# Twelve batches' block flags kept from the counting pass for the sort, and the accumulator zeroed by one transfer

## The reference

```python
xn = layernorm(x)
# graph: messages weighed by edge_weight, added up by their target node
support = xn @ gnn_weight
agg = segment_sum(edge_weight[:, None] * support[dst], src, 6250)
g = relu(agg + gnn_bias + xn)
x = x + g + linear_attention_block(xn)        # 8 heads, feed-forward 1024
x = x + top2_of_8_experts(layernorm(x))       # 256 -> 512 -> 256
```

## Time and profile before

| | us |
|---|---|
| median of 3 runs (lowest, highest) | 3451.71 (3448.81, 3453.6) |
| the profiled execution's own time | 3441.95 |
| its span | 3440.2 |
| PE busy (share of the span) | 2606.8 (76%) |
| DVE busy | 2346.8 (68%) |
| POOL busy | 2226.2 (65%) |
| ACT busy | 1248.0 (36%) |

### The profile page before, as it was taken

One profiled execution on the slowest core, in us unless ns is written; L12 is line 12 of the kernel. 1 busy time (PEld: TensorE's weight loads), 2 busy tenths in 40 slices (PEclk: granted clock), 3 DMA queues, 4 the chain that ended last, 5 costly groups with the idle time before them and its releaser, 6 DMA issues.

```text
span 3440.2 us, 46797 instructions
## 1 busy us (share of the span) xinstructions
PE 2606.8 (76%) x10870; PEld 1931.2 (56%) x10870; DVE 2346.8 (68%) x5310; ACT 1248.0 (36%) x2681; POOL 2226.2 (65%) x2110
## 2 busy tenths in 40 slices
PE   5888888667877786786786787787688754888886
PEld 2677777545544454564554565555555533776775
DVE  7999999745555656657656656656656657877863
ACT  0111111045444343344344343343344423444532
POOL 2355555577777777777777777777777733554552
PEclk9666666579889888988898998898898965999998
DMA  3111110065453543453554544445444386555445
GB/s 126 39 34 34 34 34 26 12 127 121 119 125 111 118 117 115 124 121 117 123 119 122 118 119 124 119 116 127 115 107 116 111 185 219 132 130 135 104 87 117
DMA packets 418876, 370.29 MB, mean 108 GB/s; under 512 B 248648, under 2 KB 357232, under 8 KB 418256
## 3 DMA queue, kind: packets, MB, share of 16 engines
q0 software_dynamic: 105424, 247.55, 28.0%
q1 hardware_dynamic: 304720, 110.37, 13.6%
q10 hardware_dynamic: 8496, 9.75, 0.8%
HBM read 299.09 MB, written 74.81 MB: 109 GB/s over the span
## 4 chain that ended last, share of the span: by engine, by line
PE 23%; DVE 20%; issue 12%; POOL 9%; DVEq 7%; DMA 6%; SPq 1%; ACT 1%; POOLq 0%; ACTq 0%
POOL rows L766 8%; DVE R L1567 8%; PE ps L929 6%; DVEq L1561 5%; PE ps L1003 5%; PE ps L995 4%; PE ps L1053 3%; DMA total<-y_w,zt 2%; DMA rows<-support,t_dst 2%; DVEq L1567 1%; DMA zt<-routed 1%; PE ps L963 1%; DVE xnT L1627 1%; DVE is_low L1554 1%; DVE stats L1482 1%
## 5 line engine op out<-in xcount | busy, mean ns | idle before, releaser
L766 POOL DMA_INDIRECT rows<-support,t_dst x1624 | 1598.5, 984 | 503.3 <-issue 462.7
L929 PE MATMUL ps<-rows,hot 128*128 128x256 f32 x3248 | 927.5, 435 | 377.9 <-DVE R L1567 259.8
L1567 DVE TENSOR_TENSOR R<-R,ps 128x256 f32 x1624 | 683.2, 421 | 754.3 <-DVE R L1567 474.8
L929 PEld LDWEIGHTS ps<-rows,hot 128*128 128x128 f32 x3248 | 669.8, 217 | 623.7 <-issue 383.4
L1243 ACT ACTIVATE hot<-is_low,t_w 128x128 f32<-128x128 bf16 x1624 | 689.4, 512 | 188.2 <-DVE is_low L1554 149.3
L740 POOL DMA_INDIRECT slots<-rec,st_pos x224 | 323.3, 1443 | 341.5 <-issue 194.9
L873 PE MATMUL ps<-spread,piece 128*104 128x96 bf16 x1568 | 306.2, 372 | 52.0 <-DVE spread L1476 51.8
L873 PEld LDWEIGHTS ps<-spread,piece 128*104 128x104 bf16 x1568 | 301.4, 286 | 63.8 <-DVE spread L1476 34.0
L810 POOL DMA_INDIRECT total<-y_w,zt x105 | 166.5, 1585 | 235.0 <-DMA total<-y_w,zt 177.2
L1053 PE MATMUL ps<-w_all,h_s 128*128 x1260 | 178.1, 291 | 37.2 <-DVE h_s L1894 36.3
L1053 PEld LDWEIGHTS ps<-w_all,h_s 128*128 128x128 f32 x1260 | 161.6, 192 | 63.9 <-issue 61.4
(11 more groups left out here) (261 smaller groups left out, 3350.5 us busy)
## 6 DMA issues: line engine op xcount, KB each, us to landing
rows<-support,t_dst POOLq DMA_INDIRECT x1624, 2.8
zt<-routed SPq DMA_DIRECT2D x105, 134.0 KB, 2.1
xa<-in_x SPq DMA_DIRECT2D x24, 512.0 KB
out<-total SPq DMA_DIRECT2D x1, 6250.0 KB, 21.7
xin<-in_x SPq DMA_DIRECT2D x12, 512.0 KB
support<-sup_sb ACTq DMA_DIRECT2D x12, 512.0 KB
xf<-in_x SPq DMA_DIRECT2D x12, 512.0 KB
xnb<-xb SPq DMA_DIRECT2D x12, 512.0 KB, 3.6
```

Source lines behind the costliest of these rows:

```text
L766: pool.indirect_dma_start(out=rows[h][:, j, :], out_offset=None, in_=support, in_offset=bass.IndirectOffsetOnAxis(ap=t_dst[a][:, col:col + ...
L929: last = pe.matmul(ps[q][:, t * D:(t + 1) * D], lhsT=hot[o][:, q * 2 + t, :], rhs=rows[h][:, q * 2 + t, :], start=True, stop=True)
L1567: dve.tensor_tensor(out=there, in0=there, in1=ps[q][:, t * D:(t + 1) * D], op=ALU.add).then_inc(carried, 1)
```

## The change

The flags of batches 0 to 11 are written in the counting pass to a memory of their own (`flags`), and the sort reads them there. `flag` is no longer called for them in the sort, and in the counting pass it no longer waits for TensorE for them. `over_sort` tells each turn how many of its flags are kept: 2 for turns 0 to 4, 1 for turn 5, which is now written out between two loops, 0 after it. The memset of `R` is gone; SyncE zeroes it by one transfer from `zeros`, behind the last load of `xin` and after the kept flags have been read. VectorE waits for that transfer before it first adds to `R`.

```diff
+KEPT = 12
 def over_sort(eng, chain, per, body):
-    body(0, GB, GB, False)
-    over_turns(eng, chain, 1, FULL - 1, per, lambda i: body(i, GB, GB, True))
-    body(FULL - 1, GB, 1, True)
+    half = KEPT // 2
+    body(0, GB, GB, 2)
+    over_turns(eng, chain, 1, half - 1, per, lambda i: body(i, GB, GB, 2))
+    body(half - 1, GB, GB, 1)
+    over_turns(eng, chain, half, FULL - 1, per, lambda i: body(i, GB, GB, 0))
+    body(FULL - 1, GB, 1, 0)
...
+        flags = alloc(sorting, "flags", [P, KEPT, JT * NB * CH], BF16)
+        def flagged(q, k, kept):
+            if kept:
+                return flags[:, ds(q, 1), :].rearrange("p a (j b c) -> p (a j) b c", b=NB, c=CH)
+            return onehot[k][:, :, :, :]
...
             sp.wait_ge(xn_done, FULL)
             load_x(xin, FULL, 1, x_in)
+            sp.wait_ge(op_done, KEPT)
+            sp.wait_ge(oh_read, NQ + KEPT)
+            sp.wait_ge(z_ready, 1)
+            sp.dma_start(R[:, :, :].rearrange("p a d -> p (a d)").bitcast(BF16).rearrange("p (a w) -> p a w", w=800),
+                         zeros[:, None, 0:800].to_broadcast([P, (NB + 1) * D // 400, 800])).then_inc(r_zero, 16)
...
-            pool.memset(R[:, :, :], 0.0)
...
             def add_counts(i, kept):
                 for k in range(2):
                     pe.wait_ge(oh_done, i * 2 + (k + 1))
                     for j in range(JT):
-                        last = pe.matmul(counts, lhsT=ones_bf[:, :], rhs=flat(k, j), start=False, stop=False, skip_group_check=True)
+                        last = pe.matmul(counts, lhsT=ones_bf[:, :], rhs=flat(i * 2 + k, k, j, kept), start=False, stop=False, skip_group_check=True)
...
-            def ranks(q, k):
-                pe.wait_ge(oh_done, q + (NQ + 1))
+            def ranks(q, k, kept):
+                if not kept:
+                    pe.wait_ge(oh_done, q + (NQ + 1 - KEPT))
...
-            def flag(q, k, n):
-                if not (isinstance(n, int) and n < 2):
+            def flag(q, k, n, kept=False):
+                if not kept:
                     dve.wait_ge(oh_read, n - 1)
-                dve.tensor_tensor(out=onehot[k][:, :, :, :],
+                dve.tensor_tensor(out=flagged(q, k, kept),
...
-            def pair(i, nb, nxt, owed):
-                flag(i * 2 + 1, 1, i * 2 + (NQ + 1))
+            def pair(i, nb, nxt, kept):
+                if not kept:
+                    flag(i * 2 + 1, 1, i * 2 + (NQ + 1))
                 locate(i * 2, 0)
-                position(i * 2, 0)
+                position(i * 2, 0, kept)
...
-                if nb or nxt:
+                if (nb or nxt) and kept < 2:
                     flag(i * 2 + 2, 0, i * 2 + (NQ + 2))
...
-            flag(0, 0, NQ)
...
+            dve.wait_ge(r_zero, 16)
             select(2)
```

More of the change, by code:

```diff
@@ L165, in over_sort @@
 def over_sort(eng, chain, per, body):
[L167 to L171 removed]
+    half = KEPT // 2
[4 more added lines that the diff above has]
+    body(FULL - 1, GB, 1, 0)
+    body(FULL, 1, 0, 0)
+    body(FULL + 1, 0, 0, 0)
 SORT_SEQ = 36
@@ L423, in program @@
         carried = sem("carried")
+        r_zero = sem("r_zero")
         xn2_done = sem("xn2_done")
@@ L832, in _, with flat, add_counts @@
             pe.matmul(counts, lhsT=zeros[:, 0:P], rhs=zeros[:, 0:NB * CH], start=True, stop=False)
-            def flat(k, j):
-                return onehot[k][:, j, :, :].rearrange("p b c -> p (b c)")
-            def add_counts(i):
+            def flat(q, k, j, kept):
+                return flagged(q, k, kept)[:, j, :, :].rearrange("p b c -> p (b c)")
+            def add_counts(i, kept):
                 for k in range(2):
@@ L860, in ranks @@
                 for j in range(JT):
-                    pe.matmul(ps[0][:, 0:NB * CH], lhsT=ones_bf[:, :], rhs=flat(k, j), start=(j == 0), stop=(j == JT - 1))
+                    pe.matmul(ps[0][:, 0:NB * CH], lhsT=ones_bf[:, :], rhs=flat(q, k, j, kept), start=(j == 0), stop=(j == JT - 1))
                 for j in range(JT):
-                    last = pe.matmul(ps[1][:, 0:NB * CH], lhsT=tri_bf[:, :], rhs=flat(k, j), start=(j == 0), stop=(j == JT - 1))
+                    last = pe.matmul(ps[1][:, 0:NB * CH], lhsT=tri_bf[:, :], rhs=flat(q, k, j, kept), start=(j == 0), stop=(j == JT - 1))
                 last.then_inc(oh_read, 1)
@@ L893, in turn, with pair @@
                 products(i, 0)
-            def pair(i, nb, nxt, owed):
-                ranks(i * 2 + 1, 1)
+            def pair(i, nb, nxt, kept):
+                ranks(i * 2 + 1, 1, kept >= 1)
                 if nb > 1:
@@ L902, in pair @@
                 if nb or nxt:
-                    ranks(i * 2 + 2, 0)
+                    ranks(i * 2 + 2, 0, kept == 2)
                 if nxt:
@@ L908, in _ @@
             pe.wait_ge(mixw_in, 16 * MIXW_DMAS)
-            ranks(0, 0)
+            ranks(0, 0, True)
             turn(0, GB)
@@ L1377, in _ @@
             dve.wait_ge(consts, 1)
-            def flag(q, k, n):
-                if not (isinstance(n, int) and n < 2):
+            def flag(q, k, n, kept=False):
+                if not kept:
                     dve.wait_ge(oh_read, n - 1)
-                dve.tensor_tensor(out=onehot[k][:, :, :, :],
+                dve.tensor_tensor(out=flagged(q, k, kept),
                                   in0=bkt[:, ds(q * BATCH, BATCH)].rearrange("p (j c) -> p j c", c=CH)[:, :, None, :].to_broadcast([P, JT, NB, CH]),
                                   in1=iota_b[:, None, :, :].to_broadcast([P, JT, NB, CH]), op=ALU.is_equal).then_inc(oh_done, 1)
-            for k in range(2):
-                flag(k, k, k)
-            over_turns(dve, None, 1, PAIRS, 0, lambda i: [flag(i * 2 + k, k, i * 2 + k) for k in range(2)])
+            over_turns(dve, None, 0, KEPT // 2, 0, lambda i: [flag(i * 2 + k, k, i * 2 + k, True) for k in range(2)])
+            over_turns(dve, None, KEPT // 2, PAIRS, 0, lambda i: [flag(i * 2 + k, k, i * 2 + k) for k in range(2)])
             dve.tensor_copy(out=fields[:, 2, :], in_=srci)
@@ L1447, in locate, with position @@
                                   op0=ALU.add).then_inc(idx_done, 1)
-            def position(q, k):
+            def position(q, k, kept):
                 b3 = bkt[:, ds(q * BATCH, BATCH)].rearrange("p (j c) -> p j c", c=CH)
@@ L1453, in position @@
                 dve.wait_ge(t1v_done, q + 1)
-                seq(dve.tensor_tensor(out=marks[:, :, 0:NB, :], in0=onehot[k][:, :, :, :],
+                seq(dve.tensor_tensor(out=marks[:, :, 0:NB, :], in0=flagged(q, k, kept),
                                       in1=rank[:, None, :, :].to_broadcast([P, JT, NB, CH]), op=ALU.mult))
@@ L1508, in pair @@
                     normalise(i + 1, nxt)
-                position(i * 2 + 1, 1)
+                position(i * 2 + 1, 1, kept)
                 spread_out(i * 2 + 1, 1)
             dve.wait_ge(mixw_in, 16 * MIXW_DMAS)
-            flag(0, 0, NQ)
             dve.wait_ge(x_in, 16)
```

3 lines of the change are left out of this document (2 added, 1 removed).

## The result

| us | before | changed |
|---|---|---|
| median of 10 runs each | 3451.51 (3445.84 to 3456.54) | 3442.38 (3438.56 to 3445.46) |
| ratio, 95% interval | | 0.9971 [0.9962, 0.998] |
| the profiled execution's own time | 3441.95 | 3438.62 |
| its span | 3440.2 | 3436.9 |

The change saves 9.1 us of 3451.5, or 0.3%. 3437.6 had been predicted, within 3429 to 3447. The two lines that follow are the profile page's busy table and, from its list of transfers, the new one: VectorE is busy 19.2 us less than before, and the transfer to `R` took 27.3 us.

What follows compares the result with a forecast made beforehand. VectorE was taken as the sort's limit, level with TensorE's chain in half of each turn. Savings of 6.5 + 1.4 + 6.6 + 0.4 - 0.8 = 14.1 us from 3451.7 gave 3437.6 us, range 3429 to 3447.

Steps and rivals of the forecast that it cites:

- the ring: Sort: TensorE and VectorE wait for each other, both limiting half a turn; a kept turn saves 1.65 us instead of 3.0.
- the transfer: Zeroing R in turn 10 takes 24 us, delays some six scatters about 1 us each, and loses 0.8 us.
- up to the first sort: Start, counting pass and no repeated flags of batches 0 and 1: 1.9 + 1.2 + 1.9 + 1.5 = 6.5 us saved.
- first step: Sort, first even sort to the second: 42.05 us becomes 22.4 + 18.2 = 40.6, saving 1.4 us.
- four steps: Sort, the next four even-to-even steps: each 40.8 us instead of 42.47, saving 6.6 us together.
- turn 5 written out: Sort, turn 5 no longer in a loop: 0.4 us saved, as written-out turn 0 was shorter than a looped one.
- C: Sort: TensorE's and ScalarE's chain from a turn's even sort to its odd sort, taken as 22.4 to 22.6 us.
- The address instructions: Before TensorE's matmuls on flags: covered by the preceding matmul, priced at nothing; at most 1.0 us per group of ranks.
- rival (c): Sort, turns 10 and 11: transfer served ahead of scatters, VectorE stands 12.4 us, time 3449, or 3464 if longer; chance 0.12.
- (a): Sort: VectorE stays the only limit, each of ten flags gives 1.5 us, steps 39.5, time 3430.6; chance 0.17.
- (b): Address instructions uncovered or the start's 1.9 us not saved: 4 to 6 us lost, 3442 to 3444; chance 0.14.
- (d): Sort: the change does nothing there because GpSimd or ScalarE already paces it; chance 0.02.

Runs made afterwards that it cites:

- experiment 3: Changed kernel with ScalarE normalising the next rows before counting the next batch: 3905.30 us in one run on a slower chip; last sort starts at 651.23 us.
- experiment 4: Kernel before, with ScalarE normalising before it counts: 3905.42 us in one run on a slower chip; last sort starts at 670.14 us.
- experiment 5: Kernel before with its memset of R replaced by the one transfer, no flags kept: 3446.78 us in one run, beside 3449.49 for before.
- experiment 6: Changed kernel with 6 batches kept instead of 12: 3449.42 us in one run; last sort starts at 665.27 us.
- experiment 8: Changed kernel measured again without edit: 3435.45 us, median of 5, ratio 0.9954 [0.994, 0.9967] to before.
- experiment 1: Changed kernel with R zeroed by one transfer after the sort: 3899.44 us in one run on a slower chip; last sort starts at 652.44 us.
- experiment 2: Changed kernel with the transfer to R cut in six pieces behind loads of xin: 3907.34 us in one run on a slower chip.
- experiment 7: Changed kernel with the transfer in six pieces and ScalarE normalising before counting: 3426.66 us, median of 5, ratio 0.9937 [0.9923, 0.995] to before.

## Why the prediction was right, term by term

Predicted was a gain of 14.1 us with 3437.6 as the time; measured were 9.1 us and 3442.38. The direction, the place of the gain and the ring were right, and one term, the transfer, was too small by 3.1 us. The sort accounts for 11.2 us; the other 2.1 us between it and the medians are not explained.

| term | predicted | measured in the profiles |
|---|---|---|
| up to the first sort | 6.5 | 104.19 - 97.99 = 6.2 |
| first step | 1.4 | 42.05 - 40.07 = 2.0 |
| four steps | 6.6 | 169.9 - 163.3 = 6.6 |
| turn 5 written out | 0.4 | 42.44 - 42.07 = 0.4 |
| the transfer | -0.8 | -3.9 |
| at the end of the sort | 14.1 | 11.2 |

**The ring held.** That half of each turn has two limits, and that ten flags of 1.5 us therefore give 8.6 and not 15 (8.0 had been predicted), is shown from both sides: the swap on ScalarE (experiment 3) shortens the kept turns by 1.2 us and the same swap in the kernel before (experiment 4) does nothing. The new step was put at 22.6 + 11.0 + 7.2 = 40.8 and was 22.8 + 18.05 = 40.85. The first step was the weaker reading: 22.4 was taken for its C, and it was 120.01 - 97.99 = 22.0 (the starts of turn 0's two sorts).

**The start was right in its sum and partly by luck.** The flags begin 1.6 us earlier (1.9 were expected; 0.36 us idle stands ahead of the first), and the idle 1.18 us is gone. The counting pass gave 0.6 us that the sum did not have: the twelve kept flags take (34.70 - 16.51)/12 = 1.52 us each and not 1.57. So the casts behind it begin 3.4 us earlier. The repeated flag of batch 0 gave 2.0 (1.9). That makes 5.4 at the ranks. Of these 0.7 were lost at once to the triangle's matmuls, 2.49 us against 1.79, and 1.5 came from the flag of batch 1: 6.2. The 0.7 us are TensorE's clock. Below is the busy table during the triangle's matmuls, in the kernel before and then in the changed one, with the granted clock as PEclk:

```profile
core 0: us, PE busy (x) PEld busy (x) DVE busy (x) ACT busy (x) POOL busy (x), PEclk, DMA share, GB/s
...
80.90:81.40 0.50, 0.50 (x4) 0.29 (x3) 0.00 (x0) 0.00 (x0) 0.00 (x0) 0.99 0.00 0
...
75.50:77.00 1.50, 1.50 (x5) 0.46 (x3) 0.00 (x0) 0.00 (x0) 0.00 (x0) 0.50 0.00 0
```

In both kernels TensorE had stood idle for 10.75 us shortly before, and the ranks begin at 0.50, the level of 1.2 GHz. In the kernel before it rises to 1.00, that of 2.4 GHz, at 80.9, with the triangle's matmuls half done; in the changed kernel it is still 0.50 when they end at 77.06.

What the prediction did not see is that the 1.9 us of shift and mask can be lost again to TensorE's slow first matmuls. Alone, 0.7 us of them go to longer waits for TensorE and 0.7 to the triangle (experiment 5); with six kept flags VectorE still waits 1.71 us (experiment 6), with twelve not at all. How long the slow stretch lasts differs from one execution to the next: in the changed kernel it ends near 22.4 us in the profile above and near 23.5 in experiment 8, and in experiments 1 and 6 near 21.4 and 24.3. With one trace each, the split between the causes is therefore rough.

The Trainium skill (SBUF — State Buffer, Who interferes with whom) was drawn on for these 1.9 us, that one engine waits for the whole instruction of the other at the shared port. Experiment 5 agrees: with the clear taken away and nothing else changed at that time, 1.75 and 2.11 us become 0.98 and 0.97. That the wait was for a whole instruction is not shown by itself.

**The address instructions cost nothing that could be seen,** as was put: the seven matmuls on `flags` take 2.46 to 2.49 us ahead of and in the turns, and those on `onehot` took 2.44 to 2.49. In the counting pass seven take 1.33 us on either, with the granted clock at 1.00.

**The step that failed is the transfer's 0.8 us.** Its length was nearly right (27.3 against 24). Wrong was "if their packets alternate with the long ones, I estimate 1 us more each". Scatters issued beside it land after 8 to 10 us instead of 2.4, some 6 to 8 us more each. GpSimd waits for them ahead of the next ones, so that one batch is late by much more than the 2.2 us that `st_pos` had to spare, and VectorE loses 3.9 us. The rule of the Trainium skill behind it (DMA: Bandwidth & Descriptors, Queues, rings and completion order), that a DMA engine alternates between its queues, fits the trace: scatters land at 541.5 and 553.2, while the transfer runs from 531.3 to 558.6, and rival (c), in which they land only when the transfer does, would have cost 12.4 us. But no price of a scatter follows from the rule, and the loss did not stay near a microsecond, as the prediction had concluded from it. The argument against rival (c) was weak as well: a median of 2.4 us over all 224 scatters says nothing of the few beside a load of `xin`. Experiments 1 and 2 show that the 3.9 us are the transfer's, and that six pieces of 6.3 us each cost nothing where they were placed.

**The rivals.** (a) fell: steps of 40.85, not 39.5; but it is what the kernel becomes with the swap. (b) fell: C stayed below 23 us and both operations at the start take 0.97 to 0.98, although the measured 3442.38 lies in its range of 3442 to 3444. (c) came in its form, a wait of `st_pos` on `slots` in turn 11, and with a third of its price. (d) fell.

**What stays open.** The sort ends 11.2 us earlier. The medians of the two sets of runs say 9.1 (3451.51 - 3442.38; by the interval of its ratio 6.9 to 13.1) and 14.0 (3449.49 - 3435.45; 11.4 to 20.7), and both intervals hold 11.4 to 13.1. The 11.2 us lie in the first and just below the second; by this account it is luck that 14.0 comes so near the predicted 14.1. The two profiled executions differ by 3.3 us only: their `agg<-R` is issued at 2817.1 and 2808.7, 8.4 us apart, and `out<-total` at 3418.1 and 3414.5, 3.6 apart. The stages after the sort are the same code, so their own spread from run to run is the likely reason; it was not tried by itself. In the six profiles apart from those of the first chip (the two above and experiments 5 to 8) `agg<-R` is issued 2146.4 to 2151.3 us after the last sort's start. From there to the end of the span it is 623.1 us before and 622.5 in experiment 5, both without kept flags, but 628.2 to 633.1 in the four with them. That the change costs something there is not excluded; on the first chip experiment 4, without kept flags, had the longest such stretch, 640.2 us beside 633.1 to 637.9.

## What to carry to other kernels

Where two engines hand work to and fro, removing work from the busier one pays only down to the other's chain: measure the distances between the handovers in both halves of a turn, and move what the other chain waits for (here ScalarE's order, 1.2 us a turn, by a swap of two calls) in the same change. A long transfer "beside" a stage isn't free if short transfers that someone waits for run in that stage (here 3.9 us); cut into pieces that fit into the slack, it was. Time won ahead of a handover is only worth something if the partner is ready earlier too.

## What the runs showed of the hardware

TensorE's first counting matmuls are slow after 14 us without work. The busy table by stretches of the changed kernel's start has them at 4.16 us for 13 and then at 5.50 for 35:

```profile
18.20:22.40 4.20, 4.16 (x13) 1.97 (x14) 4.20 (x3) 0.00 (x0) 0.00 (x0) 1.00 1.06 394
22.50:28.00 5.50, 5.50 (x35) 3.25 (x34) 5.50 (x5) 0.00 (x0) 0.00 (x0) 1.00 1.07 388
```

That is 0.32 and 0.16 us each, at a granted clock of 1.00, the level of 2.4 GHz, in both rows. The ranks behind 10.75 us of idleness take 2.47 and 2.49 us for seven (0.35 each), and there the granted clock is 0.50, the level of 1.2 GHz. So the first counting matmuls take what matmuls at the lower level take, while the profile shows the higher one; whether it misses the level at the program's start or something else slows them is open.

One transfer of 6400 KB inside the chip's on-core memory took 27.3 us, 234 KB per us, and kept the 16 DMA engines at 0.96 busy. Beside it an indirect scatter, 2.4 us otherwise, takes 8 to 10.

VectorE's operation that makes the flags takes 1.52 us when its results go to places of their own, and 1.57 us when it alternates between two buffers with a wait for TensorE ahead of each, although no idle time shows. Which of the two differences makes the 0.05 us was not tried.
